# 24 half-array matmuls in front of the first attention scores of a one-core decoder layer

## The reference

```
x = x + attention(layernorm(x), Wq, Wk, Wv, Wo)           # causal, RoPE, 32 heads on 8
x = x + context_attention(layernorm(x), ctx, mask)        # 64 rows of context per batch
x = x + moe(layernorm(x), router, gate_up, down)          # top 2 of 8 experts
```

## Time and profile before

| what | us |
|---|---|
| median of 3 runs | 1643.27 |
| lowest and highest of them | 1642.35, 1645.12 |
| span of the profiled execution, first to last instruction | 1640.4 |
| median less span | 2.9 |
| PE busy | 1484.6 |
| DVE busy | 1382.3 |

### The profile page before, as it was taken

How to read it: one execution, slowest core, us unless ns; L and a number is a source line. 1 busy time by engine, 2 the same in 40 slices (tenths; PEclk the granted TensorE clock), 3 DMA queues, 4 the chain that set the end, 5 groups by cost and what they waited for, 6 DMA issues and landing times. The chain is left out here.

```text
span 1640.4 us, 31332 instructions
## 1 busy us (share of the span) xinstructions
PE 1484.6 (91%) x8951; PEld 1306.0 (80%) x8951; DVE 1382.3 (84%) x3598; ACT 1057.5 (64%) x2465; POOL 849.1 (52%) x1033
## 2 busy tenths in 40 slices
PE   5789999999999899999999998688599999999994
PEld 4678888888888788888888887577489999999993
DVE  7789889889889788988988988588678988998892
ACT  3677777777777677777777777232156666666661
POOL 6667567567567547657657655256513223222321
PEclk9899999999999999999999999876589999999997
DMA  4000000000000000000000000112468888887775
GB/s 175 1 14 20 1 14 21 1 14 21 1 14 20 3 14 21 2 14 21 1 14 1 1 1 1 41 65 91 140 197 236 234 220 216 238 230 219 196 178 135
DMA packets 62032, 124.97 MB, mean 76 GB/s; under 512 B 20942, under 2 KB 21070, under 8 KB 61792
## 3 DMA queue, kind: packets, MB, share of 16 engines
q1 hardware_dynamic: 51408, 102.24, 19.7%
q0 software_dynamic: 10304, 20.59, 6.5%
q10 hardware_dynamic: 144, 0.07, 0.0%
HBM read 106.08 MB, written 24.71 MB: 80 GB/s over the span
## 5 line engine op out<-in xcount | busy, mean ns | idle before, releaser
L312 ACT ACTIVATE probs<-probs,neg_max 128x512 f32<-128x512 f32 (+3 forms) x512 | 281.7, 552 | 46.3 <-DVE neg_max L421 44.0
L545 POOL TENSOR_SCALAR probs<-probs,row_inv 128x512 f32<-128x512 f32 (+3 forms) x512 | 264.2, 534 | 42.8 <-DVE row_inv L428 42.8
L536 POOL TENSOR_TENSOR rot<-rot,sin 128x512 f32<-128x512 f32 (+1 forms) x96 | 123.7, 1289 | 305.0 <-DVE rot L440 300.6
L217 PE MATMUL bank<-ident,probs 128*128 128x128 f32 x1280 | 184.8, 275 | 59.5 <-DVE pt_lo L409 50.1
L409 DVE TENSOR_TENSOR pt_lo<-bank,pt_hi 128x512 fp32r<-128x512 f32 (+1 forms) x384 | 216.1, 590 | 25.8 <-ACT pt_hi L305 25.8
L305 ACT ACTIVATE pt_hi<-bank 128x512 fp32r<-128x512 f32 (+1 forms) x384 | 186.1, 518 | 71.8 <-PE bank L217 63.8
L421 DVE CUSTOM_DVE_ANT_0 probs<-bank,causal 128x512 f32<-128x512 f32 (+3 forms) x512 | 219.7, 481 | 10.2 <-issue 3.5
L1231 POOL DMA_INDIRECT acc<-ctx_raw,idx x46 | 74.2, 1614 | 294.5 <-ACT ctx_raw L1384 280.2
L217 PEld LDWEIGHTS bank<-ident,probs 128*128 128x128 f32 x1280 | 150.3, 141 | 94.7 <-DVE pt_lo L409 54.9
L1312 PE MATMUL bank<-xt_hi,gu_hi 128*128 128x256 f32 x736 | 208.4, 283 | 2.0 <-DVE xt_lo L409 1.5
L1312 PE MATMUL bank<-xt_lo,gu_hi 128*128 128x256 f32 x736 | 206.7, 281 | 0.0
(11 more groups left out here) (202 smaller groups left out, 3927.8 us busy)
## 6 DMA issues: line engine op xcount, KB each, us to landing
gu_raw<-in_gate_up SPq DMA_DIRECT2D x92, 512.0 KB, 3.8
dn_raw<-in_down SPq DMA_DIRECT2D x92, 256.0 KB, 3.6
w_raw<-in_wqkv SPq DMA_DIRECT2D x8, 768.0 KB, 4.2
w_raw<-in_wo_rows SPq DMA_DIRECT2D x8, 512.0 KB, 3.6
h_rows<-ln_h SPq DMA_DIRECT2D x16, 256.0 KB, 2.1
acc<-x_res SPq DMA_DIRECT2D x4, 1024.0 KB, 4.8
x_res<-in_x SPq DMA_DIRECT2D x3, 1024.0 KB, 11.2
ctx_raw<-in_ctx SPq DMA_DIRECT2D x2, 512.0 KB, 6.3
```

Of the source, the lines that this page charges most:

```text
L217: last = nc.tensor.transpose(T_BANK[u % 2][:, k * P:(k + 1) * P], probs[:, hb, P_AT[i] + j * P:P_AT[i] + (j + 1) * P], ident[:, :])
L312: nc.scalar.activation(row, row, ACT.Exp, bias=neg_max[:, hb, i:i + 1], scale=-1.0, accum_out=row_sum[:, hb, i:i + 1]).then_inc(s["exp_don ...
L536: nc.gpsimd.tensor_tensor(rot[0:rows, :], rot[0:rows, :], sin[0:rows, :], ALU.mult).then_inc(s["rot_sin"], 1)
L545: nc.gpsimd.tensor_scalar(row, row, row_inv[:, hb, i:i + 1], 0.0, ALU.mult, ALU.add).then_inc(s["pnorm_done"], 1)
```

## The change

Once, between PE's wait for `ln_lo` and the first scores, 24 matmuls are issued. Each multiplies 64 rows of `w1_hi` (128 columns, stationary) with 64 rows of `xn_hi` (512 columns, moving), starts a sum of its own and ends it. The first 12 go in pairs, one on rows 0 to 63 into bank 4 and one on rows 64 to 127 into bank 7. The other 12 are all on rows 0 to 63, in turn into bank 0 and bank 1. Nobody reads the results, and nothing waits for these matmuls by a semaphore; the next matmuls that use the banks start new sums. No other engine's list changes.

```diff
                 pe.wait_ge(s["ln_lo"], TT)
+                for halves, banks in (((0, 1), (T_BANK[1], WO_BANK)), ((0, 0), S_BANK)):
+                    for n in range(6):
+                        for k in range(2):
+                            lo_row = HD * halves[k]
+                            nc.tensor.matmul(banks[k][:, :], w1[0][lo_row:lo_row + HD, n % DC, 0:P],
+                                             xn[0][lo_row:lo_row + HD, n % DC, 0:L], start=True, stop=True)
                 pe_scores(pe, 0, 0, 0, 0)
                 pe_group(pe, 0, 0)
```

## The result

The changed kernel takes 1649.97 us (median of 7 runs, 1645.51 to 1653.82) against 1643.3 us for the kernel before in the same comparison (median of 7, 1641.82 to 1647.48). The ratio is 1.0035, with a 95% interval of 1.0021 to 1.005: slower by 5.8 us, at least 3.5 and at most 8.2 (the two medians by themselves lie 6.7 us apart). The forecast was 1647.9 in a range of 1645.7 to 1650.3. The time is inside, near the top, and the trace says that it got there another way than the likeliest case had it.

A forecast was written before the change was run, and what follows sets the result against it. It took the first block as a chain behind PE's first scores, with 0.5 us of PE-DVE slack. The late projection gave +4.5 to +5.1, taken as +4.6: span 1640.4 to 1645.0, plus 2.9 makes 1647.9 us; range 1645.7 to 1650.3.

The forecast's parts named there:

- The likeliest case: At the 24 matmuls: pairs concurrent, clock up at 50.93, eleven singles and the scores at the upper clock; +4.6 us, chance 0.50.
- the rival of +7: Lower clock through all 24 matmuls and the scores; +7 us, 1650.3 us, chance 0.07.
- if the clock rises late: One of three signs for the changed trace that would make the prediction wrong; no size given.
- the half array doesn't raise the clock: Rival: pairs 2.6 us, singles 5.1 us, scores at the lower clock; +7 us, 1650.3 us, chance 0.07.
- What comes back: After the 24: scores at the upper clock, first mask 4.8 us late, projection 4.5 us late, 5.1 with open loads.
- The first 12: Six pairs on different halves stream at once: 2.6 us at the lower clock, against 5.1 us in turn.
- The load on the same half: Last 12 matmuls: starts 0.228 us apart if the weight load is hidden, 0.28 if open; both ends kept.
- Back to 128 rows: Switch from the 64-row matmuls to the first scores: 0.1 us at most.
- What happens to it later: First block to barrier and second block: the shift passes in full, +4.5 to +5.1 us.
- No concurrency: Rival at the first 12: pairs take turns; +5.9 to +6.8 us, 1649.2 to 1650.1 us, chance 0.20.
- Given back at the second fall of the clock: Rival near 64.94: 0.6 to 1.6 us come back, +3.0 to +4.0 us; chance of an end within 3.3 us 0.20.
- Not slower: Rival at 1040 to 1190 us: shifted clock falls and rises gain the 4.6 us there; chance of faster 0.03.

The follow-up runs named there:

- the second trace of before: The unchanged kernel before, traced again; wait's end to first projection read 8.39 us, to barrier 1005.57 us, second block 585.47 us.
- 96 on one half: Kernel before plus 96 matmuls of 512 columns, all on rows 0 to 63, in place of the 24; one run 1686.99 us against 1645.73.
- 48 couples: Kernel before plus 96 matmuls in 48 couples, rows 0 to 63 and 64 to 127, in place of the 24; with the switch back they took 12.85 us.
- 64 stationary columns: Kernel before plus 96 matmuls on all 128 rows with 64 stationary columns, in place of the 24; the 96 took 23.8 us.
- the list that begins with all rows: Kernel before plus 24 matmuls on all rows, 48 on rows 0 to 63, 12 on all rows, replacing the 24; the 48 took 11 us.
- 18 on all rows: Kernel before plus 18 matmuls on all 128 rows, in place of the 24; median 1647.43 us, ratio 1.0025 (1.001 to 1.004).
- the first trace of before: The unchanged kernel before, the trace the prediction read; wait's end to first projection read 7.29 us, to barrier 1003.47 us, second block 589.16 us.
- the third: The unchanged kernel before, a third trace; wait's end to first projection read 7.34 us, to barrier 1003.69 us, second block 590.89 us.
- the second comparison: The changed kernel timed again, 12 runs, against the kernel before, 35 runs: 1648.58 against 1643.62 us, ratio 1.002 (1.0006 to 1.0035).
- the other order: The changed kernel's 24 reordered, 12 on rows 0 to 63 first, then 6 couples; block 7.98 us, first projection read after 14.65 us.
- the three first runs: Three runs of the kernel before that the prediction had, 1642.35 to 1645.12 us.

## Why the prediction was right, and where it was not

**Direction and size** came out as forecast: slower, inside the range. Part of that is luck. The forecast of +4.6 us rests on a rise of the clock that did not happen, the interval of the first comparison (3.5 to 8.2 us) holds the likeliest case and the rival of +7 alike, and the landmarks are nearer to the rival. By the prediction's own sign ("if the clock rises late") its likeliest case was wrong.

**The likeliest case was wrong in one step.** It was put as "One more at the lower clock: 50.93, where the clock has risen. Eleven at 0.228 to 0.28". The clock did not rise. All 12 on the one half ran at 1.2 GHz, 12 × 0.43 = 5.1 us instead of 2.9 to 3.5, and the scores behind them as well. The step took the rise from the kernel before as fixed in time (and read it as 3.1 us where the row gives 3.5), and did not ask what PE did meanwhile. Even for work on all rows that is not fixed: it is 5.9 us in the second trace of before. The rival for this, "the half array doesn't raise the clock", had a chance of 0.07 and +7 us; measured are 8.2 us to the first projection against the trace of before that the rival was worked out from, and 7.1 against the second, which met the place in the same state of the clock. It should have had far more. That it was the one half in use was shown by 96 on one half (41 us at the lower clock), by 48 couples and by 64 stationary columns (up after 3.7 and 3.6 us), by the list that begins with all rows, in the same state of the clock (up after 5.4 us), and by 18 on all rows, which gave the likeliest case's own numbers.

**What comes back** failed with it: the scores did not run at the upper clock. The 7.97 us to the scores lost 0.35 in DVE's slack (the first mask is 7.62 late; 0.5 was forecast), and 0.62 were added to the projection, whose way from the mask is 62.17 − 55.99 = 6.18 us against 5.56 before.

**The first 12** were right: couples at once, six in 2.6 us. **The load on the same half** is hidden, the lower of the two ends. **Back to 128 rows** costs about 0.1 us at the step, as taken, and 0.1 more at the next, at the upper clock.

**What happens to it later:** the shift was to reach the barrier whole. The changed kernel has 8.1 and 8.5 us there against the first trace of before, 7.9 and 8.2 against the third, 6.0 and 6.4 against the second. The large shifts pass too: with 96 on one half the first mask is 40.9 us later than in the first trace of before, the barrier 43.3. But the way there scatters by 2 to 3 us, and 18 on all rows brought only 2.6 of its 4.5, so "whole" is shown to within that. The time shows 5.8, and 3.3 in the second comparison. Part of the gap is that the layer norm ended 0.7 to 1.5 us earlier in the two traces of the changed kernel than in the three of before. 96 on one half, the list with all rows and the other order have the same (47.06, 46.70, 47.03); these five and the second trace of before (47.46) are the six whose last transposes took 1.11 us. As the program ahead of the place is the same in all, it looks like chance, but was not tried by itself. The rest is the second block's spread.

**The rivals.** No concurrency: refuted by the couples. Given back at the second fall of the clock: the wait and the fall are there as before. Not slower: the second block varies by 7 us, more than the 2.8 us that the three first runs let one think, and in both directions.

The rule that the prediction cited from the Trainium skill (TensorE: Matmul & The Clock Gate, "Part 3: Packing small matmuls — row/col tiling") on couples, a start some 4 ns apart, agrees with the trace at first: 0.00 to 0.01 us between the two starts at 48.11 to 51.99, but 0.03 at the end of the 48 couples. Its rule in the same section that a weight load overlaps a running matmul only where the row groups differ does not: matmuls on the same half, each with its own weight load, started 0.23 us apart.

## What to carry to other kernels

Ask of every stretch of matmuls not only how long it is but at what clock it leaves PE: a stretch on rows 0 to 63 alone behind an idle gap was paid at 1.2 GHz, and so were the scores behind it. Put work on all rows, or couples on both halves, where the clock has to come up; once it is up, half-height matmuls did not bring it down in 11 us. And where runs scatter by more than the effect, compare distances between landmarks in several traces of both kernels, and sort the traces by the clock that they bring to the place.

## What the runs showed of the hardware beyond that

- The clock stayed at 1.2 GHz through 41 us of gapless matmuls on 64 rows, but stayed at 2.4 GHz through 11 us of the same when it was up before. With 64 stationary columns on 128 rows it rose after 3.6 us. In the four traces with singles on rows 0 to 63 right ahead of the scores it rose 4.3 to 5.1 us after the first matmul on all rows.
- The two halves of the array behaved like separate queues. With 12 singles on the lower half ahead of 6 couples, the two `w_lo` rows at 51.04 are one matmul at 51.04 and, by their joint 0.80 us less the 0.62 of one, one at 51.22. The first is the tenth single in its pace. The other, with a `w_lo`, started before the eleventh single (a `w_hi`, 51.47), though in the order of the program every `w_lo` after the tenth single stands behind that one; by the pace it is the first on the upper half (the row doesn't name the half). The first couple's lower half started at 52.32. So the upper half ran some 1.1 us ahead, and the two matmuls of a couple did not start together in this list.
- A second trace of one and the same kernel had its clock rise 5.9 us after PE's start instead of 3.5, at the same place in the program. In it the last transposes ahead had run at the lower clock (1.11 us for 0.68).
